# Shared expert unrolled, its products regrouped, its routing in pieces, and the expert-weight splits moved to pairs 3 to 14

## The reference, cut to what matters

```python
logits = einsum('bsd,de->bse', x, Wr) * SCALE               # x is the layernorm of x1; 8 experts
_, idx = top_k(logits + rb, 2)
w = softmax(take_along_axis(logits, idx))                   # the two experts' shares
# routed experts, for the two chosen:
h = (x @ W1[e]) * silu(x @ W3[e]);  expert_out = h @ W2[e]  # 256 -> 512 -> 256
# shared expert, for every token:
hs = (x @ Ws1) * silu(x @ Ws3);     out = out + hs @ Ws2
```

## Time and profile before

| | |
|---|---|
| median of 3 runs | 1294.36 us (1294.14 to 1297.22) |
| the profiled execution | 1297.05 us, its span 1295.3 us |
| PE, matmuls | 1098.8 us busy, 85% |
| PE, weight loads | 829.3 us, 64% |
| DVE | 843.1 us, 65% |
| POOL | 685.3 us, 53% |
| ACT | 622.1 us, 48% |
| mean granted clock of TensorE | 0.954 of full speed |
| DMA | 137.19 MB, mean 106 GB/s |

### The profile page before, as it was taken

The page is one execution under the profiler, slowest core; times in us unless marked ns, Lnnn a source line. Parts: engine busy times, 40 slices in busy tenths (PEclk is TensorE's granted clock), DMA queues, the critical chain, the costliest instruction groups (busy, mean ns, idle before and its releaser), DMA issues. The chain is left out here.

```text
span 1295.3 us, 27552 instructions
## 1 busy us (share of the span) xinstructions
PE 1098.8 (85%) x8532; PEld 829.3 (64%) x8533; DVE 843.1 (65%) x1791; ACT 622.1 (48%) x1483; POOL 685.3 (53%) x794
## 2 busy tenths in 40 slices
PE   4877877888647999799999999997498889699998
PEld 2555555555436787466666656654387777599997
DVE  3999899888747666444444444454588887566664
ACT  3666666666623555233233213322344444566664
POOL 7677677766306766499999566001656650100000
PEclk9999899999868999899999999998699999799999
DMA  1422222222154888735441101112334330111110
GB/s 33 127 91 99 76 100 89 85 85 94 62 191 162 285 274 269 225 136 185 155 154 57 57 25 57 57 53 69 107 115 120 121 106 33 50 50 50 49 49 34
DMA packets 113782, 137.19 MB, mean 106 GB/s; under 512 B 12368, under 2 KB 102448, under 8 KB 111920
## 3 DMA queue, kind: packets, MB, share of 16 engines
q1 hardware_dynamic: 104480, 101.63, 24.5%
q0 software_dynamic: 9232, 34.67, 7.8%
HBM read 83.83 MB, written 52.43 MB: 105 GB/s over the span
## 5 line engine op out<-in xcount | busy, mean ns | idle before, releaser
L253 POOL TENSOR_TENSOR bd<-T,hmask 128x1024 f32<-128x1024 f32 x64 | 150.5, 2372 | 6.9 <-ACT T L371 6.9
L360 ACT ACTIVATE pr<-S,nmx 128x128 f32<-128x128 f32 x512 | 139.3, 396 | 3.9 <-DVE nmx L284 3.9
L956 ACT CAST hT<-HT 128x512 f16<-128x512 f32 x72 | 42.1, 585 | 198.7 <-PE HT L914 198.7
L411 PE MATMUL S<-bd,T 128*128 128x512 f32 x256 | 126.4, 618 | 0.0
L893 PE MATMUL YB<-wm,hT 128*128 x864 | 106.5, 273 | 3.6 <-DVE hT L979 3.6
L893 PE MATMUL Ge<-wm,xT 128*128 x432 | 107.6, 386 | 1.0 <-DVE xT L984 1.0
L893 PE MATMUL Ue<-wm,xT 128*128 x432 | 105.7, 381 | 0.0
L893 PEld LDWEIGHTS YB<-wm,hT 128*128 128x128 f16 x864 | 84.4, 98 | 29.3 <-issue 4.5
L290 DVE SCALAR_TENSOR_TENSOR pT<-PT,pT 128x1024 f16<-128x1024 f32 x64 | 77.6, 1213 | 35.8 <-ACT pT L352 34.6
L1729 PE MATMUL H<-T6s,wm 128*128 128x256 f16 x768 | 96.5, 277 | 1.2 <-DVE T6s L1668 1.2
L1194 POOL DMA_INDIRECT yg<-ys_d,slot x64 | 66.0, 1032 | 58.3 <-POOLq L858 41.2
(11 more groups left out here) (248 smaller groups left out, 2571.1 us busy)
## 6 DMA issues: line engine op xcount, KB each, us to landing
stage<-in_L_ffn_W_dram SPq DMA_DIRECT2D x24, 512.0 KB, 6.1
xs_d<-zeros SPq DMA_DIRECT2D x36, 256.0 KB, 2.4
xe<-xs_d SPq DMA_DIRECT2D x72, 128.0 KB, 2.1
ys_d<-ye SPq DMA_DIRECT2D x72, 128.0 KB, 1.7
bw<-in_L_ffn_up_weights_dram POOLq DMA_DIRECT2D x7, 1024.0 KB, 5.8
bw<-_L_ffn_down_weights_dram POOLq DMA_DIRECT2D x7, 1024.0 KB, 5.6
xb<-in_x_dram SPq DMA_DIRECT2D x32, 128.0 KB, 2.1
cb<-in_ctx_dram SPq DMA_DIRECT2D x32, 128.0 KB, 2.2
```

The source lines that it names most:

```text
L253: nc.gpsimd.tensor_tensor(out=bd[:, a, c, :, :], in0=T0[:, a, C + c:C + c + 1, :].broadcast_to([P, HH, P]), in1=hmask[:, :, :], op=ALU.mul ...
L360: last = nc.scalar.activation(pr[:, h, i, :], S[h][:, i, :], ACT.Exp, bias=nmx[:, h, i:i + 1])
L411: last = nc.tensor.matmul(S[h][:, i:i + 4, :], T0[:, k % 2, h, :], bd[:, k % 2, h, i:i + 4, :], start=True, stop=True)
```

## The change

The hardware loop is gone: the second block is written out for all pairs. Besides that:

- PE does up(t,0), up(t,1), down(t-1,0), down(t-1,1). Its two counting matmuls stand in iteration 1 behind the up products.
- DVE's iteration is: product(t,0), rest of the input (t+1), rest(t,0), product(t,1), rest(t,1), the splits of pair t, and both adds of pair t-1. The product waits for `s_fl` as well.
- The routing is cut in pieces: the first choice before pair 0; the second choice after rest(0,0); the gate logits at the end of iteration 0; counts and slots in iteration 1, in front of the adds; the shares and the tiles' experts in iteration 2. Exp is at the beginning of ACT's iteration 1, behind the Silus of pair 0.
- POOL waits for SLOTS_AT (the slots are there) in place of ROUTED_AT, and takes the slot numbers from `slot` itself.
- The splits go to pairs 3 to 14, two each, behind the work of the pair. SP issues the two matrices of split(t+2) at the end of its round t. `stage` is used in turn by n % 3, as before by kind.

The diff's core (PE's `up` and `down` change only in their conditions and indices):

```diff
-
-one = lambda e: bass.ds(e, 1)
+pairs = lambda a, p: a[2 * p:2 * p + 2, :, :].rearrange("t p n -> p t n")
+NW = 3 * E
+SPLIT = 3
+split = lambda t: range(max(0, 2 * (t - SPLIT)), max(0, min(NW, 2 * (t - SPLIT) + 2)))
+assert sum(len(split(t)) for t in range(NP)) == NW
...
     @block.sync
     def _(sp):
+        def weight(n):
+            if n >= 3:
+                sp.wait_ge(s_wl, 2 * (n - 2))
+            w = (W3, W1, W2)[n % 3]
+            sp.dma_start(stage[:, n % 3, :].rearrange("p (c n) -> p c n", n=w.shape[2]),
+                         w[n // 3, :, :].rearrange("(c p) n -> p c n", p=P)).then_inc(s_st[n % 3], 16)
+
         sp.dma_start(rbb[:, :], rb.rearrange("(o e) -> o e", o=1).broadcast_to([P, E])).then_inc(s_rb, 16)
-
-        def body(t, k):
-            if onp(t + 1):
-                for n2, kind, e in matrices(t + 1, (k + 1) % 4):
-                    if due(n2 - 4):
-                        sp.wait_ge(s_wl, n2 - 4)
-                    w = (W3, W1, W2)[kind]
-                    sp.dma_start(stage[:, kind, :].rearrange("p (c n) -> p c n", n=w.shape[2]),
-                                 w[one(e), :, :].rearrange("o k n -> (o k) n").rearrange(
-                                     "(c p) n -> p c n", p=P)).then_inc(s_st[kind], 16)
-            if onp(t + 4):
-                if due(2 * t + 2):
+        for t in range(-4, NP + 1):
+            if 0 <= t + 4 < NP:
+                if t >= 0:
                     sp.wait_ge(s_ad, 2 * t + 2)
-                sp.dma_start(hs[:, k, :, :, :].rearrange("p t c n -> p t (c n)"),
-                             h1T_d[bass.ds((t + 4) * 2, 2), :, :].rearrange("t p n -> p t n")
-                             ).then_inc(s_hl[k], 16)
-                sp.dma_start(xr[:, k, :, :],
-                             x1_d[bass.ds((t + 4) * 2, 2), :, :].rearrange("t p n -> p t n")
-                             ).then_inc(s_hl[k], 16)
-            if onp(t):
+                sp.dma_start(hs[:, t % 4, :, :, :].rearrange("p t c n -> p t (c n)"),
+                             pairs(h1T_d, t + 4)).then_inc(s_hl[t % 4], 16)
+                sp.dma_start(xr[:, t % 4, :, :], pairs(x1_d, t + 4)).then_inc(s_hl[t % 4], 16)
+            if 0 <= t < NP:
                 sp.wait_ge(s_ad, 2 * t + 2)
-                sp.dma_start(acc_d[bass.ds(t * 2, 2), :, :].rearrange("t p n -> p t n"),
-                             ao[:, k % 2, :, :]).then_inc(s_ast[k % 2], 16)
-            if onp(t + 3):
-                a = (k + 3) % 4
-                if due((t + 3 - a) * 16):
-                    sp.wait_ge(s_scat[a], (t + 3 - a) * 16)
-                sp.dma_start(ht[:, a, :, :], h1_d[bass.ds((t + 3) * 2, 2), :, :].rearrange("t p n -> p t n")
-                             ).then_inc(s_ht[a], 16)
-
-        steps(sp, *RANGE3, body)
+                sp.dma_start(pairs(acc_d, t), ao[:, t % 2, :, :]).then_inc(s_ast[t % 2], 16)
+            if 0 <= t + 3 < NP:
+                a = (t + 3) % 4
+                if t >= 1:
+                    sp.wait_ge(s_scat[a], 64 * ((t + 3) // 4))
+                sp.dma_start(ht[:, a, :, :], pairs(h1_d, t + 3)).then_inc(s_ht[a], 16)
+            for n in split(t + 2):
+                weight(n)
         for j in range(2):
             sp.wait_ge(s_ast[j], 16 * (NP // 2))
...
-        def body(t, k):
-            up(t, k, 0)
-            down(t - 1, k + 1, 0)
-            up(t, k, 1)
-            down(t - 1, k + 1, 1)
-            if isinstance(t, int) and t == 0:
-
+        for t in range(NP + 1):
+            up(t, 0)
+            up(t, 1)
+            if t == 1:
                 pe.wait_ge(s_i, 5)
                 pe.wait_ge(s_v, MASK_AT)
                 nc.tensor.matmul(R[:, 0, :, :], upper[:, :], mask[:, :, :], start=True, stop=True)
                 nc.tensor.matmul(R[:, 1, :, :], ones[:, :], mask[:, :, :], start=True,
                                  stop=True).then_inc(s_mm, 1)
-
-        steps(pe, 0, *RANGE3[1:], body)
+            down(t - 1, 0)
+            down(t - 1, 1)
...
     @block.scalar
     def _(act):
-        def body(t, k):
-            if isinstance(t, int) and t == 0:
+        for t in range(-1, NP):
+            if t == 1:
                 act.wait_ge(s_v, GATE_AT)
                 nc.scalar.activation(gl[:, :, :], gl[:, :, :], ACT.Exp).then_inc(s_e, 1)
-            if onp(t + 1):
-                a = (k + 1) % 4
-                act.wait_ge(s_hl[a], (t + 1 - a) * 8 + 32)
-                if due(2 * t):
+            if t + 1 < NP:
+                a = (t + 1) % 4
+                act.wait_ge(s_hl[a], 32 * ((t + 1) // 4 + 1))
+                if t >= 1:
                     act.wait_ge(s_up, 2 * t)
                 nc.scalar.mul(hp[:, a % 2, HI, :, :, :], hs[:, a, :, :, :], XS).then_inc(s_xh3, 1)
-            if onp(t - 1):
-                for n2, kind, e in matrices(t - 1, (k - 1) % 4):
-                    act.wait_ge(s_st[kind], loads(t - 1, (k - 1) % 4))
-                    take_wait(nc.scalar)
-                    nc.scalar.mul(wm[:, kind, one(e), HI, :].rearrange("p o n -> p (o n)"),
-                                  stage[:, kind, :], WS).then_inc(s_wh, 2)
-            if onp(t):
+            if t >= 0:
                 for h in range(2):
                     act.wait_ge(s_up, 2 * t + h + 1)
-                    if due(2 * t - 1 + h):
+                    if t >= 1:
                         act.wait_ge(s_ml, 2 * t - 1 + h)
                     nc.scalar.activation(sg[:, h, :, :], G[h][:, :, :], ACT.Silu,
                                          scale=1 / (XS * WS)).then_inc(s_sl, 1)
                     act.wait_ge(s_ml, 2 * t + h + 1)
-                    if due(2 * t - 2):
+                    if t >= 2:
                         act.wait_ge(s_dn, 2 * t - 2)
-                    nc.scalar.copy(hh[:, k % 2, HI, 2 * h:2 * h + 2, :], hf[:, h, :, :]).then_inc(s_fh, 1)
-
-        steps(act, -4, *RANGE3[1:], body)
+                    nc.scalar.copy(hh[:, t % 2, HI, 2 * h:2 * h + 2, :], hf[:, h, :, :]).then_inc(s_fh, 1)
+            for n in split(t):
+                act.wait_ge(s_st[n % 3], 16 * (n // 3 + 1))
+                nc.scalar.mul(wm[:, n % 3, n // 3, HI, :], stage[:, n % 3, :], WS).then_inc(s_wh, 2)
...
+        def choose_first():
 
             dve.wait_ge(s_rb, 16)
             dve.wait_ge(s_i, 5)
             link(TT(sel[:, :, :], logits[:, :, :], over_b(rbb[:, :]), ALU.add))
-            for j in range(TOPK):
-                link(RED(top[:, :], sel[:, :, :], AX.X, ALU.max))
-                link(TT(t0[:, :, :], sel[:, :, :], over_e(top[:, :]), ALU.is_ge))
-                link(TT(t0[:, :, :], t0[:, :, :], over_b(revi[:, :]), ALU.mult))
-                link(RED(top[:, :], t0[:, :, :], AX.X, ALU.max))
-                link(TT(oh[:, j, :, :], over_b(revi[:, :]), over_e(top[:, :]), ALU.is_equal))
-                if j + 1 < TOPK:
-                    link(TS(t0[:, :, :], oh[:, j, :, :], -1.0, 1.0, ALU.mult, ALU.add))
-                    link(TT(sel[:, :, :], sel[:, :, :], t0[:, :, :], ALU.mult))
-                    link(TS(t0[:, :, :], oh[:, j, :, :], -3.0e38, None, ALU.mult))
-                    link(TT(sel[:, :, :], sel[:, :, :], t0[:, :, :], ALU.add))
+            choose(0)
+            link(TS(t0[:, :, :], oh[:, 0, :, :], -1.0, 1.0, ALU.mult, ALU.add))
+            link(TT(sel[:, :, :], sel[:, :, :], t0[:, :, :], ALU.mult))
+            link(TS(t0[:, :, :], oh[:, 0, :, :], -3.0e38, None, ALU.mult))
+            link(TT(sel[:, :, :], sel[:, :, :], t0[:, :, :], ALU.add))
+
+        def choose_second():
+
+            choose(1)
             link(TT(mask[:, :, :], oh[:, 0, :, :], oh[:, 1, :, :], ALU.add))
             assert done[0] == MASK_AT, done
...
                 dve.wait_ge(s_sl, 2 * t + h + 1)
-                if due(2 * t - 1 + h):
+                if t >= 1:
                     dve.wait_ge(s_fh, 2 * t - 1 + h)
+                    dve.wait_ge(s_fl, 2 * t - 1 + h)
                 nc.vector.scalar_tensor_tensor(hf[:, h, :, :], U[h][:, :, :], ES / (XS * WS),
                                                sg[:, h, :, :], ALU.mult, ALU.mult).then_inc(s_ml, 1)
 
...
-        def add(t, k, j):
-            if onp(t):
+        def add(t, j):
+            if t >= 0:
                 dve.wait_ge(s_dn, 2 * t + j + 1)
...
-        def body(t, k):
-            if onp(t + 1):
-                a = (k + 1) % 4
-                dve.wait_ge(s_xh3, t + 2)
-                nc.vector.scalar_tensor_tensor(hp[:, a % 2, LO, :, :, :], hs[:, a, :, :, :], XS,
-                                               hp[:, a % 2, HI, :, :, :], ALU.mult,
-                                               ALU.subtract).then_inc(s_xl3, 1)
-            if onp(t - 1):
-                for n2, kind, e in matrices(t - 1, (k - 1) % 4):
-                    dve.wait_ge(s_wh, n2 + 2)
-                    nc.vector.scalar_tensor_tensor(
-                        wm[:, kind, one(e), LO, :].rearrange("p o n -> p (o n)"), stage[:, kind, :], WS,
```

(117 more changed lines are left out.)

36 lines of the change are left out of this document (19 added, 17 removed).

## The result

The changed kernel takes 1332.3 us (median of 4 runs, 1330.9 to 1339.1), the kernel before 1294.6: 3.0% slower, ratio 1.030 with the interval 1.028 to 1.032, or 38 us more. The forecast was 1334, in a range of 1318 to 1352.

The account below looks back on a forecast made before the run. PE bound the old steady part; the new load loop would set the pace: 412.5 + 11 x 12.3 + 10.7 + 8.3 = 566.8 against 527.15, +39.7 us, giving 1334 us against the median, range 1318 to 1352.

Parts of the forecast that it names:

- The loop: Weight splits: each round's loads must land, be scaled and finished before the next issue; 12.3 us a round, 11.0 to 14.2.
- the quick end: Shortest round by the earlier trace: second matrix 9.2 us after the hs issue plus 3.25 behind it, 12.45 us.
- my discount: Earlier weight issue (2.0 us, not 3.3) and queues left idle shorten the round a little; 12.3 us taken.
- The last rounds: End of the block: a last round of 10.7 us without hs and xr, then 8.3 us for iterations 15 and 16.
- A(12): A(t) is the moment DVE has done the second add of pair t, which SP awaits before issuing round t.
- The start, up to A(1): From block start to pair 1's second add: 412.5, the same as before, change 0 within -3 to +2 us.
- The 2.6 that I named as a possibility: At the start, A(1) would be 2.6 us earlier if neither extra table load waits for its data.
- Priced at nothing: PE's order and clock, dropped waits and copies, POOL's scatters (through by about 560) and later stages: no cost.
- Hidden loads: Rival: loads are covered and DVE or PE sets the pace, 8.1 us a pair, 1285 us; chance 0.06.
- the short loop: Rival: the loop exists but takes 9.5 to 11.0 us because queues are drained, about 1312 us; chance 0.08.
- The low clock: Rival: PE, pausing each round, falls to the low clock for good, some 16 us a pair, 1380 us; chance 0.03.
- my estimate of the round: From the skill's bandwidth: 5.9 us for 2.1 MB plus 2.0 for issue and completion, loop 11.2, loss 26 us.

Follow-up runs that it names:

- e1: The changed kernel with SP issuing the matrices of split(t+3), not split(t+2), at the end of round t: 1279.25 us, ratio 0.987.
- e8: The changed kernel with the old split schedule (1294.25 us with early loads), but its matrices issued at the end of SP's round: 1392.43 us, ratio 1.075.
- e2: The changed kernel with the two matrices issued first in SP's round, ahead of hs, xr, acc and ht: 1293.96 us, ratio 0.999.
- e5: As e1, with ACT's Exp moved from the beginning of its iteration 1 to its end, behind the Silus of pair 1: 1273.9 us, ratio 0.984.
- e7: As e1, with adds before the routing's pieces, counts in iteration 1, slots in 2, experts, shares and Exp in 15: 1275.1 us, ratio 0.983.
- e3: The changed kernel with DVE's two adds put in front of the two weight splits: 1292.03 us, ratio 0.997.

## Why the prediction was right, point by point

- **The loop** was the right mechanism: e1 opens it, e8 makes it elsewhere. The round was 12.67 us in the mean of eleven, against 12.3; the quick end of the earlier trace rows (12.45) was nearer than my discount. 11 x 0.37 = +4.1 us against the sum. Of the discount's two effects the first did come, the matrices were issued 2.0 us after `hs` and not 3.3, but it bought nothing in the rounds shown: the first matrix was there 7.8 after `hs` both times. The second, emptier queues, did not shorten the landing: 6.0 in the median, just as before (6.1), though the DMA engines' share had fallen from 0.82 to 0.63. What does shorten it is to take the four transfers of its own round from in front of it, 1 MB (e2). The 9.2 that I took from the earlier trace rows as the quickest landing is an upper bound: that row at 467.22 has no idle time before it, so ACT was still busy with the first matrix. That the quick end fits is in part luck.
- **The last rounds.** A(12) to A(13) was 10.1 (10.7 in the sum), from there to the last add 7.6 (8.3): -1.3 together.
- **The start, up to A(1)**, is the step that failed. It was to be 412.5, within -3 to +2, and was 405.7, 6.8 earlier and outside the 409 to 415 that I had set. Pair 0's first product began at 375.1 and not at 379.1. Of these 4.0 us, 0.4 are the block's earlier start (first issue at 364.13, before 364.56), 1.1 the first input, which ACT could take 4.3 us after its issue and not 5.4 (why, no run shows), 1.2 the granted clock (1.54 for twelve matmuls where the earlier trace rows has 2.77), and 1.3 Silu's first table load, which was already done. Pair 1's product came at 386.9 and not 392.6, 1.7 more: 1.3 of it is Exp's load, which ran ahead of its data. The remaining 1.1 are spread over the pieces and adds. I had priced all three table loads on the path. The 2.6 that I named as a possibility were Exp's and the second Silu's; of these only Exp's left the path, for Silu's at 384.88 ran directly in front of its Silu and DVE waited 2.8 us there. The other load that cost nothing was the first. The rows of the changed kernel, and below them the first input's of the kernel before:

```profile
364.55 0.44 SPq L535 DMA_DIRECT2D hs<-h1T_d  x1
...
368.86 0.63 ACT L604 ACTIVATE hp<-hs 128x512 f16<-128x512 f32 x1 [7.88 <-DMA xr<-x_d]
...
371.88 1.28 ACT L610 ACT_TABLE_LOAD   x1
...
372.80 1.54 PE L563 MATMUL U<-hp,wsm 128*128 128x256 f16 x12
...
374.38 0.60 ACT L610 ACTIVATE sg<-G 128x512 f32<-128x512 f32 x1 [1.22 <-PE U L563]
...
381.16 1.28 ACT L598 ACT_TABLE_LOAD   x1
...
384.09 0.26 ACT L598 ACTIVATE gl<-gl 128x64 f32<-128x64 f32 x1 [1.65 <-DVE gl L665]
384.25 0.61 ACT L604 ACTIVATE hp<-hs 128x512 f16<-128x512 f32 x1
384.88 1.28 ACT L610 ACT_TABLE_LOAD   x1
386.18 0.60 ACT L610 ACTIVATE sg<-G 128x512 f32<-128x512 f32 x1
...
386.86 0.69 DVE L725 SCALAR_TENSOR_TENSOR hf<-U,sg 128x512 f32<-128x512 f32 x1 [2.81 <-ACT sg L610]
```

```profile
364.98 0.43 SPq L543 DMA_DIRECT2D hs<-h1T_d  x1
...
370.40 0.63 ACT L620 ACTIVATE hp<-hs 128x512 f16<-128x512 f32 x1 [8.99 <-DMA xr<-x_d]
```

- Together: -6.8 + 4.1 - 1.3 = -4.0, which is 562.9 measured against 566.8 for the last add. That the total came out only 2 us from the forecast is in part luck: the start erred by -6.8 and the loop by +4.1.
- **Priced at nothing.** PE's idle time did hide the low clock: the down products took 4.34 us where e5's took 2.78, and the adds waited for them twice in the whole block, 2.2 us together. The last scatter was issued at 552.7, ten us before the last add. Both as argued. PE was busy 74% of 412 to 560 us, not two thirds, because part of its work ran at the low clock.
- **The rivals.** Hidden loads, the faster side, need another place of the issue: e1 is that kernel, and takes 1279, where the rival's sum said 1285, from a start 6.8 us later. A round as short as the short loop's, or shorter, is e2's (9.2 us, 1294 us), but by the order within the round and not by drained queues. The low clock did not stay: 0.90 in the mean.
- **Rule and row.** The Trainium skill ("ScalarE: Activation LUTs", What ACT_TABLE_LOAD costs) has a drain of 1.38 us with each switch. The rows above disagree: the load at 384.88 starts 0.02 us after the scaling in front of it ends, and Silu starts 0.02 us after the load's end, at 386.18. By the Trainium skill's bandwidth ("DMA: Bandwidth & Descriptors", Specifications, 358 GB/s of HBM a core) my estimate of the round was 11.2; the measured mean is 12.67. The rate itself is near what e1 reaches, 342 GB/s at a DMA share of 1.00; the estimate's other part, 2.0 us for issue and completion, the page gives for one load on GpSimd's path (Anatomy of one DMA), and these are six in a row from SP. Which of the two parts is too small here, no run separates.

## What to carry to other kernels

When loads are issued behind a wait for a pair's last operation, look up in which iteration they are used, and whether that iteration's last operation is what the next issue waits for. If so, each turn costs issue, landing and all that follows, and no engine's busy share tells it: 12.7 us a pair here against 7.9 with the loop open. One round of lead, with the buffers there were, was worth 53 us; and a wait in the issuing engine's stream holds what is issued behind it (9 us in e7, which cost PE 4.8), so put the loads that are urgent in front of the ones that may wait.

## What the runs showed of the hardware that I had not expected

A table load of ACT does not wait for the data of its activation: in the changed kernel it ran at 371.88, 2.5 us before the Silu whose matmuls it stood in front of, and at 381.16, 2.9 us before Exp. In both places ACT was idle and the change of table cost nothing. At 384.88 Silu's data were there, and the 1.28 us were on the path.

How long a 512 KB load takes from issue to landing depends on what was issued in front of it: at nearly the same DMA share over 412 to 500 us, 0.90 and 0.91, the median is 4.8 us where the matrices come first in the round (e2) and 7.1 where they come last (e3). But the order alone doesn't fix it, nor does the share: last in the round, it is 6.0 in the changed kernel (0.66), 6.3 in e1 (1.00) and 7.1 in e3. In e1 the second matrix also goes out apart from the rest, because it waits for its buffer. What separates these three, no run here shows.
